# A two-block graph attention kernel on one core: another order in the opening, and two steps moved in the second head

## What is computed

```python
h = (x @ W1).reshape(n, 8, 768)                 # W1: 768 x 6144
e = leaky_relu(alpha_src[src] + alpha_dst[dst]) # alpha: h dotted with a_src, a_dst
alpha = softmax of e over the edges of each dst
h = elu(segment_sum(h[src] * alpha, dst) + b1)
out = gat_conv(h, src, dst, W2, ...)            # W2: 6144 x 768, one head
x = layernorm(x + out)
```

## Time and profile before

| | |
|---|---|
| median of 3 runs | 361.6 us (361.49 to 362.41) |
| the profiled execution, its own time | 363.34 us |
| its span | 361.5 us |
| TensorE busy | 349.8 us (97%) |
| ACT busy | 218.7 us |
| DVE busy | 213.7 us |
| POOL busy | 242.5 us |
| mean granted TensorE clock | 0.993 of full speed |

### The profile page before, as it was taken

One profiled execution on the slowest core, in us unless ns is written; L12 is line 12 of the kernel. 1 busy time (PEld: TensorE's weight loads), 2 busy tenths in 40 slices (PEclk: granted clock), 3 DMA queues, 4 the chain that ended last, 5 costly groups with the idle time before them and its releaser, 6 DMA issues.

```text
span 361.5 us, 6079 instructions
## 1 busy us (share of the span) xinstructions
PE 349.8 (97%) x2058; PEld 300.3 (83%) x2060; DVE 213.7 (59%) x545; ACT 218.7 (60%) x376; POOL 242.5 (67%) x163
## 2 busy tenths in 40 slices
PE   7999999899999999999999999999999999999994
PEld 3888888788988988998898898888767888788883
DVE  4999872436418235553641834455687797953776
ACT  5897595637754864673775486467276867264601
POOL 2389659483883967669397496856256898687911
PEclk9999999899999999999999999999999999999999
DMA  7888967356556546574654665567162657337002
GB/s 248 284 301 227 397 229 258 130 176 173 175 163 198 166 170 188 169 244 130 222 178 136 214 172 174 188 167 245 57 199 94 181 190 196 131 113 233 5 2 87
DMA packets 24544, 65.15 MB, mean 180 GB/s; under 512 B 1952, under 2 KB 3024, under 8 KB 24528
## 3 DMA queue, kind: packets, MB, share of 16 engines
q1 hardware_dynamic: 20864, 55.02, 45.7%
q10 hardware_dynamic: 3664, 9.92, 10.0%
HBM read 64.15 MB, written 0.79 MB: 180 GB/s over the span
## 4 chain that ended last, share of the span: by engine, by line
PE 79%; DMA 4%; DVE 4%; POOL 4%; issue 4%; ACT 3%; DVEq 0%; POOLq 0%; SPq 0%
PE ps L1006 56%; PE ps L1296 9%; PE ps L1094 6%; POOL ring_lo L370 3%; DMA raw<-in_L_gnn_W 3%; PE ps L1128 2%; PE ps L1360 2%; DMA b_rows<-in_L_gnn_b 1%; PE ps L1073 1%; ACT ring_hi L357 1%; PE ps L1058 1%; DVE stats L1740 1%; DVE ps L1960 1%; POOL x_sb L634 1%; DVE z L1967 1%
## 5 line engine op out<-in xcount | busy, mean ns | idle before, releaser
L370 POOL TENSOR_TENSOR ring_lo<-raw,ring_hi 128x768 fp32r<-128x768 f32 x92 | 167.1, 1850 | 75.6 <-ACT ring_hi L357 75.6
L357 ACT ACTIVATE ring_hi<-raw 128x768 fp32r<-128x768 f32 x96 | 77.4, 839 | 40.0 <-PE ps L1006 28.9
L386 POOL TENSOR_TENSOR ring_lo<-raw,ring_hi 128x512 fp32r<-128x512 f32 (+1 forms) x40 | 59.4, 1512 | 20.3 <-ACT ring_hi L379 20.2
L1006 PE MATMUL ps<-ring_hi,zT_hi 128*128 128x256 f32 (+1 forms) x256 | 69.3, 346 | 0.9 <-ACT zT_hi L808 0.9
L1006 PE MATMUL ps<-ring_lo,zT_hi 128*128 128x256 f32 (+1 forms) x256 | 67.1, 337 | 0.0
L1006 PE MATMUL ps<-ring_hi,zT_lo 128*128 128x256 f32 (+1 forms) x256 | 66.8, 338 | 0.0
L1513 DVE CUSTOM_DVE_ANT_0 e<-ps,att 128x768 f32<-128x768 f32 x38 | 34.2, 953 | 49.0 <-PE ps L1006 49.0
L1006 PE MATMUL ps<-ring_hi,xT_hi 128*128 128x512 f32 x192 | 52.0, 347 | 2.1 <-DVE zT_lo L1662 1.8
L1006 PE MATMUL ps<-ring_hi,xT_lo 128*128 128x512 f32 x192 | 50.5, 341 | 0.0
L1006 PE MATMUL ps<-ring_lo,xT_hi 128*128 128x512 f32 x192 | 50.5, 339 | 0.0
L1006 PEld LDWEIGHTS ps<-ring_hi,zT_hi 128*128 128x128 f32 x256 | 42.0, 189 | 7.1 <-ACT zT_hi L808 1.6
(11 more groups left out here) (172 smaller groups left out, 545.1 us busy)
## 6 DMA issues: line engine op xcount, KB each, us to landing
raw<-in_L_gnn_W SPq DMA_DIRECT2D x54, 768.0 KB, 4.4
raw<-in_L_gnn_Wr SPq DMA_DIRECT2D x8, 768.0 KB, 4.5
att<-in_L_gnn_a_src ACTq DMA_DIRECT2D x10, 384.0 KB, 3.7
att<-in_L_gnn_a_dst ACTq DMA_DIRECT2D x10, 384.0 KB, 4.9
raw<-in_L_gnn_W SPq DMA_DIRECT2D x4, 384.0 KB, 5.1
x_sb<-in_x SPq DMA_DIRECT2D x3, 256.0 KB, 4.9
rows_hc<-in_L_gnn_b SPq DMA_DIRECT2D x1, 512.0 KB, 7.8
rows_hc<-in_L_gnn_g SPq DMA_DIRECT2D x1, 512.0 KB, 8.6
```

The lines of the kernel that those rows point to most:

```text
L357: eng.activation(slot_hi(c), raw_chunk(c), ACT.Copy).then_inc(hi_done, 1)
L370: eng.tensor_tensor(slot_lo(c), raw_chunk(c), slot_hi(c).bitcast(F32), ALU.subtract)\
L386: eng.tensor_tensor(ring_lo[:, q["ring_at"]:q["ring_at"] + w], raw[:, q["raw_group"], q["raw_at"]:q["raw_at"] + w], ring_hi[:, q["ring_at" ...
L1006: last = pe.matmul(ps[:, at + to:at + to + hi - lo], a, b[:, lo:hi], start=start and n == 0 and to != D, stop=stop and n == PASSES - 1, sk ...
```

## The change

Opening:
- src and dst are loaded as 32 rows of 128 numbers each (512 bytes to a row) into 64 partitions, where before each of 128 partitions got 32 numbers (128 bytes) twice. DVE makes them float, TensorE turns them (64 columns) in the midst of chunk (0, 0), and DVE copies the result out of PSUM.
- The first part of x is rounded in two halves, each released by its own signal. The first product of chunks (0, 0) and (0, 2) waits for the high part alone, the second for the low part. The parts of x stand in other banks, and the third waits until the first has been read.
- Of eight wide dummy matmuls seven stay and two narrow ones are added; the two between the turning of x and the first product go.
- b1 is issued ahead of ACT's first wait, and turned ahead of chunk (0, 2).
- Slices 20 to 31 of the one-hots carry no weight any more and are made by two wide comparisons; the weight is multiplied into the steps of `late_steps`, six of which use the opposite comparison with the opposite sign.

Heads 0 and 1:
- In `elu(0)` on DVE the second tile of the dot with a_dst of head 1 moves behind the first third.
- `att_for(2)` moves on ACT from ahead of the rounding of phase 3 to between that and `elu(1)`. The loop keeps its order.

```diff
@@ sync
-            sp.dma_start(edges[:, 0, :], src.rearrange("(p t) -> p t", p=P)).then_inc(edges_loaded, 16)
-            sp.dma_start(edges[:, 1, :], dst.rearrange("(p t) -> p t", p=P)).then_inc(edges_loaded, 16)
+            sp.dma_start(edge_rows[0:ET, :], src.rearrange("(t p) -> t p", p=P)).then_inc(edges_loaded, 16)
+            sp.dma_start(edge_rows[ET:2 * ET, :], dst.rearrange("(t p) -> t p", p=P)).then_inc(edges_loaded, 16)
@@ scalar
             act.activation(rstd[:, 0:1], half[:, :], ACT.Exp)
+            act.dma_start(b1_rows[:, :], b0_b1.rearrange("(t p) -> t p", p=P)).then_inc(b1_loaded, 16)
...
             split_hi(act, FIRST_PHASE, 0, reused=False)
-            act.dma_start(b1_rows[:, :], b0_b1.rearrange("(t p) -> t p", p=P)).then_inc(b1_loaded, 16)
-            input_hi(0)
+            input_hi(0, 1, 1)
+            input_hi(1, 1, 2)
...
                 exps(h, (1, 0))
-                after_exps(h, last)
-
-            def after_exps(h, last=False):
                 att_for(h + 1, last)
+                after_exps(h)
+                elu(h)
+
+            def after_exps(h):
                 for c in range(4):
                     split_hi(act, 2 * h + 1, c)
                 weights_hi(h)
                 for c in (4, 5):
                     split_hi(act, 2 * h + 1, c)
-                elu(h)
...
             after_exps(1)
+            att_for(2)
+            elu(1)
@@ tensor
-            keep_warm(8, PROJ)
+            keep_warm(7, PROJ)
+            keep_warm(2, PROJ, P)
...
             transpose_x(0)
-            keep_warm(2, PROJ + 2 * BANK)
             for c in range(CH):
-                if c == 1:
+                if c == 2:
                     pe.wait_ge(b1_loaded, 16)
...
                 if c in (0, 2):
-                    pe.wait_ge(xT_hi_done, c // 2 + 1)
-                    chunk(FIRST_PHASE, c)
-                    for passes in (FIRST_TWO, LAST_ONE):
+                    pe.wait_ge(xT_hi_done, c + 1)
+                    pe.wait_ge(hi_done, c + 1)
+                    for passes in ((0,), (1,), LAST_ONE):
+                        if passes == (1,):
+                            chunk(FIRST_PHASE, c)
                         if passes is LAST_ONE:
                             pe.wait_ge(xT_lo_done, c // 2 + 1)
+                        if passes is LAST_ONE and c == 0:
+                            pe.wait_ge(edges_cast, 1)
+                            pe.wait_ge(iota_cast, 2)
+                            pe.transpose(ps[:, EDGES_AT:EDGES_AT + 2 * ET], edge_rows_f[:, :],
+                                         ident[0:2 * ET, 0:2 * ET]).then_inc(edges_ps, 1)
@@ vector
             split_lo(dve, FIRST_PHASE, 0)
+            dve.wait_ge(edges_loaded, 32)
+            dve.tensor_copy(edge_rows_f[:, :], edge_rows[:, :]).then_inc(edges_cast, 1)
             input_lo(0)
-            dve.wait_ge(edges_loaded, 32)
-            dve.tensor_copy(edges_f[:, :, :], edges[:, :, :]).then_inc(edges_cast, 1)
-            dve.wait_ge(edges_cast, 1)
+            dve.wait_ge(edges_ps, 1)
+            dve.tensor_copy(edges_f[:, :, :].rearrange("p s t -> p (s t)"), ps[:, EDGES_AT:EDGES_AT + 2 * ET])\
+               .then_inc(edges_placed, 1)
+            dve.wait_ge(edges_placed, 1)
...
-                    dve.tensor_scalar(step(t), iota[:, :], edges_f[:, 0, t:t + 1], -0.5, ALU.is_ge, ALU.add)\
-                       .then_inc(step_dve_done, 1)
+                    dve.tensor_scalar(step(t), iota[:, :], edges_f[:, 0, t:t + 1], weight_of[:, t:t + 1],
+                                      ALU.is_lt if t >= BELOW_FROM else ALU.is_ge, ALU.mult).then_inc(step_dve_done, 1)
...
-            hots(0, ET)
+            hots(0, ACT_STEPS)
+            for first, end in PLAIN:
+                plain_hots(first, end)
...
-            dots(1, a_d, 1, a_dst_done)
-            elu(0)
+            dots(1, a_d, 1, a_dst_done, tiles=(0,))
+            elu(0, between=lambda: dots(1, a_d, 1, a_dst_done, tiles=(1,)))
```

More of the change, by code:

```diff
@@ L139, in build_gnn @@
         iota = sb("iota", [P, 1 + N], BF16)
-        edges = sb("edges", [P, 2, ET], I32)
+        edge_rows = sb("edge_rows", [2 * ET, P], I32)
+        edge_rows_f = sb("edge_rows_f", [2 * ET, P])
         edges_f = sb("edges_f", [P, 2, ET])
@@ L1184, in count_edges @@
                 for t in range(ET):
-                    pe.wait_ge(hot_done, t + 1)
+                    pe.wait_ge(hot_done, t + 1 if t < ACT_STEPS else ACT_STEPS + sum(first <= t for first, _ in PLAIN))
                     if t < ACT_STEPS:
@@ L1456, in _, with plain_hots @@
             dve.tensor_copy(iota_ps, iota_i).then_inc(iota_cast, 1)
+            def plain_hots(first, end):
+                at = (first % per_home) * 2 * N
+                home = hot_homes[first // per_home][:, at:at + (end - first) * 2 * N]
+                shape = [P, end - first, P]
+                dve.tensor_tensor(home.rearrange("p (t n) -> p t n", n=2 * N)[:, :, 0:P],
+                                  iota_ps[:, 1:1 + P].rearrange("p (t n) -> p t n", t=1).to_broadcast(shape),
+                                  row_of[:, first:end].rearrange("p (t n) -> p t n", n=1).to_broadcast(shape),
+                                  ALU.is_equal).then_inc(hot_done, 1)
             def hots(first, end):
@@ L1642, in weights_tiles_lo, with elu @@
                        .then_inc(wt_lo_done, 1)
-            def elu(h):
+            def elu(h, between=None):
                 for q in range(3):
+                    if q == 1 and between is not None:
+                        between()
                     if q >= 1:
```

44 lines of the change are left out of this document (26 added, 18 removed).

## The result

The changed kernel takes 360.28 us (median of 20 runs, 359.44 to 362.14), the kernel before on the same chips 361.96 us (20 runs, 361.36 to 363.99). The ratio is 0.9948, with an interval from 0.9932 to 0.9964: faster by a little, 1.7 us between the medians (1.9 by the ratio), where 4.0 were forecast. 360.28 is in the range, just inside its upper end, and 2.7 us above the forecast of 357.6.

The account below looks back on a forecast made before the run. TensorE, busy nearly all the time, was taken as the bound, so only its idle and slow-clock stretches could be won. 0 + 0.52 + 1.96 + 1.55 = 4.0 us off 361.6 gave 357.6 us, range 356.7 to 360.3.

Parts of the forecast that it names:

- The load of 7.1 us falls to 4.4: Third raw load of phase 3, without attention loads beside it; ends TensorE's wait near 63 us, worth 1.96 us.
- 0.52 us at zT_hi: Near 43 us: moving the dot lets ACT round earlier; TensorE gains 0.52 of 0.54 us idle time.
- The spare time of 0.6 us: Near 62 us: elu(1)'s low part ready at 61.8, TensorE wanting it at 62.4, so no wait.
- their upper bound of 0.5: ACT ahead of elu(1): delay by the two moved load issues, between nothing and 0.5 us, taken as 0.15.
- I assume they share the stall: Whole kernel: the median runs were taken to lose what the profiled execution lost, so 361.6 − 4.0 = 357.6 us.
- the clock term: TensorE from 66.42 us: pairs every 0.64 us, not 0.35, at the lower clock; 1.55 us to win.
- The opening is worth 0: Up to chunk (0, 3): the microsecond won at chunk (0, 1) is waited away; bounds −0.2 and +0.6 us.
- the 0.74 forecast: DVE in the opening: twelve late steps with a second value per partition, 62 ns more each, +0.74 us.
- Rival 4: Opening: idle TensorE leaves the clock low some 3 us, delaying edges and DVE by 1 us; 358.6 us, 8%.
- gaps of 0.97 and 0.54 us left no mark: Argument against a low clock in the opening: idle gaps at 9.59 and 43.57 us had not slowed TensorE.
- Wide comparisons win nothing: DVE one-hots behind chunk (0, 3): about 2 us saved only covers their 0.9 us later start.
- rival 3: Opening: edges landing in 5.4 us, not 3.3, put DVE 1.3 us later at chunk (0, 3); 358.9 us, 10%.

Follow-up runs that it names:

- heads: Kernel before with both edits in heads 0 and 1 (moved dot, moved attention loads) and the old opening: 359.23 us, ratio 0.9938.
- a_warm: Changed kernel with the old dummies (eight wide ahead of x, two wide behind its turning): 359.92 us, ratio 0.9961.
- a_fill_oldsteps: Changed kernel with b1 loaded late, nine wide dummies ahead of x's turning, and the old late steps and one-hots: 359.78 us, ratio 0.995.
- dots_only: Kernel before with only the a_d dot of head 1 moved behind the first third of elu(0): 361.43 us, ratio 0.9971.
- a_oldsteps: Changed kernel with the late steps and one-hots of the kernel before: 359.97 us, ratio 0.9957.

## Why the prediction was half right

- *The load of 7.1 us falls to 4.4, TensorE no longer waits for zT_lo, 0.52 us at zT_hi.* Right in mechanism and in each number of the first profile: 4.3 us for the load (4.3 to 4.9 over all kernels that move the attention loads), no wait, no slow stretch, 4.2 us behind chunk (0, 3). The spare time of 0.6 us was too high: zT_lo is done at 63.86 in the changed kernel and TensorE asks at 64.16. In heads the moved issues cost 0.68 us on ACT, above their upper bound of 0.5 (0.15 was taken), and TensorE waited 0.48.
- *"The median of the runs is 361.6, by 1.7 us below that execution; I assume they share the stall and take 361.6 − 4.0 = 357.6 us."* This is the step that failed. The difference of 1.7 us was the clock term itself: executions of the lower group have the wait but not the slow clock. The term of 1.55 us isn't in the median, and the wait was 1.41 in the second profile, where 1.96 was taken. What is left is 0.52 + 1.41 = 1.9 us; behind chunk (0, 3) 2.2 were measured, and no row here accounts for the other 0.3. The price of the clock was read rightly from rows, but from one execution, and taken off the median of others.
- *The opening is worth 0 (bounds −0.2 and +0.6).* In the lower group this was nearly right: chunk (0, 3) starts 10.11 us behind x's turning, in the kernel before 9.95 to 9.97. The late steps cost DVE 0.73 us, as the 0.74 forecast (the Trainium skill's formula, VectorE: DVE Perf Modes, The TRN2 errata, has no term for them, and here the measurement decides), and TensorE idles ahead of chunks (0, 1) and (0, 3) for ring_lo, as said. But b1's early load delays x by 0.2 to 0.3 us, a cost with no term in the sum. Together chunk (0, 3) starts 0.4 to 0.5 us later than in the second profile of before, outside the bounds.
- *Rival 4, the clock low in the opening, price 1 us, chance 8%.* It happened in 12 of the 24 executions of the changed kernel, at a price of 1.5 us and not 1 (361.0 to 361.3 against 359.7 to 359.8). (The 12 are by their time; of the five profiled, three had the slow start.) The second half of its mechanism stands as written: slow products delay the edges, and the edges DVE. The first half doesn't: with the two dummies back the slow start was there (a_warm), and the idle time ahead of x does not decide it. The size was off because the slow stretch is 4 us long or more, and not 3. What starts it is open. The reason against it ("gaps of 0.97 and 0.54 us left no mark") took gaps in the midst of work for evidence on the start. The page of the Trainium skill named beside it (TensorE: Matmul & The Clock Gate, What's actually happening) says that the rise after the start differs from run to run, and by it some runs would pay and some not. These runs show that, with a larger spread than the half microsecond either way that the page gives: in the changed kernel the full pitch is there at 5.4 us or comes after 9. It should have had more weight.
- *Wide comparisons win nothing.* Wrong by a little: in this opening DVE is so late that the old one-hots held the count for 0.42 us (a_fill_oldsteps).
- *Edges late (rival 3).* No: issue to landing was 3.4 to 3.7 us in the profiles of the changed kernel.

The two groups give the sum again. Lower against lower: 361.5 − 2.2 + 0.4 = 359.7; upper group of the changed kernel: + 1.5 = 361.2. Half of the executions in each group make the median of 360.28 a value that no execution has.

## What to carry to other kernels

Compare the time of the profiled execution with the list of runs before taking a term from it: a term that accounts for just their difference, as the slow clock did here (1.55 of 1.7 us), may be missing in most of them; the mean granted clock of each run, where it is listed, can tell. Count each issue that is moved ahead of a wait as traffic beside the load that the engine waits for next, and look at its length on the issuing engine in more than one profile. And where the first real products follow dummies, check the spacing of equal matmuls in several executions: a slow start cost 0.4 us in one opening here and 1.5 in the other.

## What the runs showed of the hardware

- Behind one and the same wait TensorE ran on at 1.2 GHz for 3 us in one execution (granted clock 0.58, idle 1.81) and not in two others (granted clock 1.00, idle 1.25 and, with the moved dot, 1.99). The longest idle time was among the unharmed.
- In the first 10 us TensorE can run at the pitch of 1.2 GHz while the granted clock reads 1.00. In the changed kernel it lasted to 9 us and beyond or wasn't there from x's turning on, with the same idle time ahead (0.81 and 0.80). Over all kernels x's turning was slow behind no idle time (dots_only) and fast behind 1.29 us (a_oldsteps).
- Two broadcasts of 384 KB in flight stretch a load of 768 KB beside them from 4.3 to 4.9 us to 6.5 to 7.2.
- The second of these issues took 0.45 to 0.51 us on ACT in its old place and 0.58 to 1.83 in the new one; the longest kept the next operation waiting for 0.68 us (heads).
- A step on DVE with a second value per partition (and a multiplication for an addition) takes 61 ns more.

Open: what decides between the slow and the fast start, and why a slow one ends sooner in the old opening. No kernel here changed the idle time ahead of x's turning alone, with enough runs to count.
